# Signs taken in the copy out of PSUM, quarters added by TensorE, in a kernel of window attention and product keys

## What is computed

```
x = L0_attn_hidden_states
xn = _layernorm(x, axis=-1)
s = _L0_attn_ref(xn, ...)
g = _silu(_L0_ffn_ref(xn, L0_ffn_Wq, L0_ffn_keys, L0_ffn_W_down, L0_ffn_W_up))
x = x + s * g
```

```
sx, ix = jax.lax.top_k(sim[0], TOPK)
sy, iy = jax.lax.top_k(sim[1], TOPK)
all_scores = (sx[..., :, None] + sy[..., None, :]).reshape(b, n, HEADS, TOPK * TOPK)
scores, pk_indices = jax.lax.top_k(all_scores, TOPK)
h = jax.nn.gelu(jnp.einsum('bnd,bnhkd->bnhk', x, W_down[pk_indices]), approximate=False)
h = h * jax.nn.softmax(scores, axis=-1)
return jnp.einsum('bnhk,bnhkd->bnd', h, W_up[pk_indices])
```

## Time and profile before

| | us |
|---|---|
| time, median of 3 runs | 278.73 |
| lowest and highest | 277.35, 278.85 |
| the profiled execution, its time | 277.19 |
| its span in the profile | 275.4 |

### The profile page before, as it was taken

How to read it: one execution, slowest core, us unless ns; L and a number is a source line. 1 busy time by engine, 2 the same in 40 slices (tenths; PEclk the granted TensorE clock), 3 DMA queues, 4 the chain that set the end, 5 groups by cost and what they waited for, 6 DMA issues and landing times.

```text
span 275.4 us, 7038 instructions
## 1 busy us (share of the span) xinstructions
PE 237.8 (86%) x1562; PEld 176.2 (64%) x1562; DVE 261.0 (95%) x1715; ACT 234.9 (85%) x1048; POOL 225.9 (82%) x344
## 2 busy tenths in 40 slices
PE   7799689897989988988898889988998899898891
PEld 7456343685668666765676577657765776587780
DVE  5899999999999999999999999999999999998985
ACT  2553866989899999999989999999999999998953
POOL 7889701467588979998999889988998899889972
PEclk9999999999899999999999999999999999999997
DMA  7930000000000000100000000100010001000102
GB/s 179 281 80 1 2 0 0 2 1 0 5 0 0 5 0 1 38 6 0 2 12 31 1 0 2 42 0 5 0 39 4 1 0 40 2 1 4 38 4 76
DMA packets 11228, 6.23 MB, mean 23 GB/s; under 512 B 1457, under 2 KB 10674, under 8 KB 11186
## 3 DMA queue, kind: packets, MB, share of 16 engines
q1 hardware_dynamic: 9858, 5.12, 7.0%
q10 hardware_dynamic: 1328, 0.66, 1.1%
HBM read 3.67 MB, written 2.10 MB: 21 GB/s over the span
## 4 chain that ended last, share of the span: by engine, by line
POOL 29%; PE 29%; ACT 22%; issue 14%; DVE 5%; POOLq 0%; ACTq 0%; DVEq 0%
POOL past L487 4%; PE scratch L1662 4%; PE sim L1570 4%; POOL squareT L502 4%; ACT prob L847 3%; POOL drop L509 3%; POOL wgt L515 3%; PE s_bank L1764 3%; PE s_bank L1758 2%; ACT gap L769 2%; ACT spare L866 2%; PE t_bank L1588 2%; PE s_bank L1553 2%; POOL wgt L523 2%; ACT side L739 2%
## 5 line engine op out<-in xcount | busy, mean ns | idle before, releaser
L1215 DVE MAX8 top<-rest 128x8 f32<-128x40 f32 x512 | 57.4, 191 | 0.1
L1165 DVE MAX8 top<-sim 128x8 f32<-128x32 f32 x496 | 54.0, 184 | 0.0
L847 ACT ACTIVATE prob<-drop 128x50 f32<-128x50 f32 x224 | 51.5, 254 | 0.0
L847 ACT ACTIVATION_READ_ACCUMULATOR prob<-drop 128x1 f32 x224 | 46.9, 211 | 0.0
L502 POOL TENSOR_TENSOR squareT<-sideT 100x512 bf16<-100x512 bf16 x31 | 32.6, 1050 | 4.8 <-ACT sideT L757 4.8
L487 POOL TENSOR_TENSOR past<-gap,last 128x400 f32<-128x400 f32 x31 | 26.8, 864 | 9.5 <-DVE last L1239 9.5
L1570 PE MATMUL sim<-sim_w,xT_all 128*128 128x512 f32 x64 | 33.9, 611 | 0.5 <-ACT xT_all L794 0.5
L509 POOL TENSOR_TENSOR drop<-gap,out_by 128x400 f32<-128x400 f32 x30 | 31.0, 1033 | 1.2 <-ACT out_by L746 1.2
L1588 PE MATMUL t_bank<-gaps_of,topT 128*128 128x200 f32 x128 | 30.1, 359 | 2.0 <-ACT topT L762 2.0
L515 POOL TENSOR_TENSOR wgt<-prob,rden 128x400 f32<-128x400 f32 x30 | 25.7, 856 | 5.9 <-DVE rden L1157 5.9
L1239 DVE MAX8 last<-slot_gap 128x8 f32<-128x22 f32 x256 | 24.4, 169 | 1.1
(11 more groups left out here) (295 smaller groups left out, 755.7 us busy)
## 6 DMA issues: line engine op xcount, KB each, us to landing
out<-y_sb SPq DMA_DIRECT2D x7, 256.0 KB, 2.3
x_sb<-in_L_attn_hidden_states SPq DMA_DIRECT2D x2, 256.0 KB, 3.8
fwq_sb<-in_L_ffn_Wq ACTq DMA_DIRECT2D x2, 256.0 KB, 5.6
x_sb<-in_L_attn_hidden_states SPq DMA_DIRECT2D x1, 512.0 KB, 5.3
wc_sb<-in_L_attn_Wc SPq DMA_DIRECT2D x1, 256.0 KB
out<-last_y SPq DMA_DIRECT2D x2, 128.0 KB, 1.9
wo_in<-in_L_attn_Wo SPq DMA_DIRECT2D x1, 192.0 KB
keys_sb<-in_L_ffn_keys ACTq DMA_DIRECT2D x1, 128.0 KB, 3.3
```

Source lines behind the costliest of these rows:

```text
L847: last = nc.scalar.activation(prob[d][:, h, :], drop[:, h, :], ACT.Exp, scale=-1.0, accum_out=den[d][:, h:h + 1])
L1165: last = nc.vector.max(top[n % 3][:, v, 0:8], sim_bank[n % 2][:, bass.ts(v, KEYS)])
L1215: last = nc.vector.max(top[n % 3][:, v, 8:16], rest[:, v, :])
```

## The change

The sign is no longer taken on its own. GpSimd writes the differences as bf16, TensorE turns the differences themselves, and ScalarE's copy out of PSUM takes the sign (Sign in the place of Copy). side_of goes, with its 32 calls in ScalarE's order and its semaphore. Since the differences stay in use until TensorE has turned them, past_of waits for sideT_ready where it waited for side_done. For the last tile, last_past_of reads the gaps from the PSUM bank in which they still lie (t_bank), and not from their copy; last_squares squares the signs in SBUF and waits for them, where it squared the copy's source in PSUM.

add_quarters goes, with its 28 calls and its semaphore. add_halves has two buffers in turn, and expert_weights adds the two halves that are left with two fp32 matmuls into the same place of PSUM, as it did before for tile 28.

```
-        past = sb("past", [P, HEADS, CANDS])
-        side = sb("side", [P, HEADS, CANDS], BF16)
+        past = sb("past", [P, HEADS, CANDS], BF16)
-        wgt4 = sb("wgt4", [P, HEADS // 2, CANDS])
-        wgt2 = [sb(f"wgt2_{i}", [P, 2, CANDS]) for i in range(2)]
+        wgt4 = [sb(f"wgt4_{i}", [P, HEADS // 2, CANDS]) for i in range(2)]
...
                 pool.wait_ge(last8_done, n + 1)
                 if n >= 1:
-                    pool.wait_ge(side_done, n)
+                    pool.wait_ge(sideT_ready, n)
...
             def add_halves(n):
                 pool.wait_ge(wgt_done, n + 1)
-                w = wgt[n % 2]
-                nc.gpsimd.tensor_tensor(wgt4[:, :, :], w[:, 0:HEADS // 2, :], w[:, HEADS // 2:HEADS, :],
-                                        ALU.add).then_inc(wgt4_done, 1)
-
-            def add_quarters(n):
-                pool.wait_ge(wgt4_done, n + 1)
                 if n >= 2:
                     pool.wait_ge(c_ready, n - 1)
-                nc.gpsimd.tensor_tensor(wgt2[n % 2][:, :, :], wgt4[:, 0:2, :], wgt4[:, 2:4, :],
-                                        ALU.add).then_inc(wgt2_done, 1)
+                w = wgt[n % 2]
+                nc.gpsimd.tensor_tensor(wgt4[n % 2][:, :, :], w[:, 0:HEADS // 2, :], w[:, HEADS // 2:HEADS, :],
+                                        ALU.add).then_inc(wgt4_done, 1)
...
-            def side_of(n):
-                if n < TILES - 1:
-                    act.wait_ge(past_done, n + 1)
-                else:
-                    act.wait_ge(last_past, 1)
-                if n >= 1:
-                    act.wait_ge(sideT_ready, n)
-                nc.scalar.activation(side[:, :, :], past[:, :, :], ACT.Sign).then_inc(side_done, 1)
...
-                    nc.scalar.activation(last_sideT[0:TWO, :], t_bank[0:TWO, :], ACT.Copy).then_inc(sideT_out, 1)
+                    nc.scalar.activation(last_sideT[0:TWO, :], t_bank[0:TWO, :], ACT.Sign).then_inc(sideT_out, 1)
...
-                nc.scalar.activation(sideT[0:TWO, :], f_bank[0:TWO, :], ACT.Copy).then_inc(sideT_out, 1)
+                nc.scalar.activation(sideT[0:TWO, :], f_bank[0:TWO, :], ACT.Sign).then_inc(sideT_out, 1)
...
             def last_squares():
-                nc.scalar.activation(last_squareT[0:TWO, :], t_bank[0:TWO, :], ACT.Square).then_inc(last_square, 1)
+                act.wait_ge(sideT_out, TILES)
+                nc.scalar.activation(last_squareT[0:TWO, :], last_sideT[0:TWO, :], ACT.Square).then_inc(last_square, 1)
...
             def last_past_of(m):
                 dve.wait_ge(last8_done, m + 1)
-                dve.wait_ge(side_done, m)
-                nc.vector.tensor_tensor(past[:, :, :], gap[m % 4][:, :, :],
+                dve.wait_ge(sideT_ready, m)
+                nc.vector.tensor_tensor(past[:, :, :],
+                                        t_bank[:, 0:HEADS * CANDS].rearrange("p (h c) -> p h c", c=CANDS),
                                         last8[m % 2][:, :, 7:8].to_broadcast([P, HEADS, CANDS]),
                                         ALU.subtract).then_inc(last_past, 1)
...
             def transpose_sides(n):
-                pe.wait_ge(side_done, n + 1)
+                if n < TILES - 1:
+                    pe.wait_ge(past_done, n + 1)
+                else:
+                    pe.wait_ge(last_past, 1)
...
-                    last = mm(dst[0:TWO, bass.ts(k, P)], side[:, 2 * k:2 * k + 2, :].rearrange("p h c -> p (h c)"),
+                    last = mm(dst[0:TWO, bass.ts(k, P)], past[:, 2 * k:2 * k + 2, :].rearrange("p h c -> p (h c)"),
                               ident16[:, :], start=True, stop=True)
...
-                if n < TILES - TB:
-                    pe.wait_ge(wgt2_done, n + 1)
-                    last = nc.tensor.transpose(o, wgt2[n % 2][:, :, :].rearrange("p h c -> p (h c)"), ident[:, :])
+                if n <= TILES - TB:
+                    pe.wait_ge(wgt4_done, n + 1)
+                    w, heads = wgt4[n % 2], HEADS // 2
...
+                for h in range(0, heads, 2):
+                    last = mm(o, w[:, h:h + 2, :].rearrange("p h c -> p (h c)"),
+                              ident[:, :], start=(h == 0), stop=(h == heads - 2))
                 last.then_inc(c_ready, 1)
```

More of the change, by code:

```diff
@@ L277, in program @@
         topT_ready, topT_out, gap_ready, gap_out = (sem(n) for n in ("topT_ready", "topT_out", "gap_ready", "gap_out"))
-        slot_gap_done, last8_done, past_done, side_done = (
-            sem(n) for n in ("slot_gap_done", "last8_done", "past_done", "side_done"))
+        slot_gap_done, last8_done, past_done = (sem(n) for n in ("slot_gap_done", "last8_done", "past_done"))
         ahead_done, count_q_done, count_full, count_in = (
@@ L286, in program @@
         half_out = sem("half_out")
-        wgt_done, wgt4_done, wgt2_done, c_ready, c_out = (
-            sem(n) for n in ("wgt_done", "wgt4_done", "wgt2_done", "c_ready", "c_out"))
+        wgt_done, wgt4_done, c_ready, c_out = (
+            sem(n) for n in ("wgt_done", "wgt4_done", "c_ready", "c_out"))
         last_past, last_square, last_kept, last_wgt, blocks_scaled = (
@@ L615, in turn @@
                     add_halves(n - 4)
-                    add_quarters(n - 4)
                     square_of(n - 2)
@@ L819, in _ @@
             take_topT(1)
-            side_of(0)
             take_gaps(1)
@@ L991, in turn @@
                     take_topT(n - 1)
-                    side_of(n - 2)
                     if b >= 2:
@@ L1054, in _ @@
             take_sides(0)
-            side_of(1)
             unit(0, U_KW, [(kw[:, :], 0, bk_sb, 1.0)])
@@ L1070, in _ @@
             out_by_of(TILES - 3)
-            side_of(TILES - 2)
             unit(B - 1, U_VW, [(vw[:, :], 0, bv_sb, 1.0)])
@@ L1076, in _ @@
             window_exps(B - 1, range(LAST, TB))
-            side_of(TILES - 1)
             block_exps(B - 1)
@@ L1627, in expert_weights @@
                 o = dst[0:TWO, bass.ts(n % TB, P)]
-                if n < TILES - TB:
-                    pe.wait_ge(wgt2_done, n + 1)
-                    last = nc.tensor.transpose(o, wgt2[n % 2][:, :, :].rearrange("p h c -> p (h c)"), ident[:, :])
-                else:
[L1632 to L1643, removed]
+                if n <= TILES - TB:
+                    pe.wait_ge(wgt4_done, n + 1)
+                    w, heads = wgt4[n % 2], HEADS // 2
+                elif n < TILES - 1:
+                    pe.wait_ge(wgt_done, n + 1)
+                    w, heads = (wgt if n < TILES - LAST else last_wgts)[n % 2], HEADS
+                else:
+                    pe.wait_ge(last_wgt, 1)
+                    w, heads = last_wgts[n % 2], HEADS
+                for h in range(0, heads, 2):
+                    last = mm(o, w[:, h:h + 2, :].rearrange("p h c -> p (h c)"),
+                              ident[:, :], start=(h == 0), stop=(h == heads - 2))
                 last.then_inc(c_ready, 1)
```

## The result

The changed kernel takes 276.31 us (median of 22 executions, 276.11 to 279.26), the kernel before in the same comparison 278.64 us (22 executions, 277.22 to 280.07). The ratio is 0.9931 with a 95% interval of 0.9913 to 0.9949, or -2.3 us between the medians where -1.0 was forecast. The lowest times lie 1.1 us apart and the two profiled executions 0.66 us (276.53 and 277.19). So the first question is which of these is the change's.

A forecast was written before the change was run, and what follows sets the result against it. A lap of waits round ScalarE, TensorE and GpSimd, not VectorE, was taken to bound the kernel. Laps -0.1, way in -0.4 and tail -0.5 gave -1.0 us: median 277.7 us, own range 276.6 to 278.5, full range 275.0 to 279.9.

The forecast's parts named there:

- The lap: Main loop, one batch element in four turns round ScalarE, TensorE and GpSimd: -0.02 us each, -0.1 us over six.
- Sign at turn 1: ScalarE in turn 1: without side_of, pT_win comes 0.43 us earlier.
- Stall at turn 0: TensorE at turn 0: transpose_sides no longer waits for ScalarE, -0.25 us, between 0.19 and 0.30.
- expert_weights in turn 1: TensorE's unbroken stretch in turn 1: the extra matmuls adding the quarters cost +0.33 us.
- In turn 3: TensorE between the count and the block scores: the extra matmuls of expert_weights cost +0.33 us.
- VectorE's floor: Main loop: VectorE's busy time of 27.52 us per 28.15 us period; its 0.63 us of waiting limits the gain.
- the freed loop: Rival for the main loop: TensorE's extra 0.66 us hides, VectorE alone binds, 274.0 us; chance 0.18, partly or in full.
- The way in: Loop's first turns: the 0.51 us wait for side_of goes, part is given back; -0.4 us, between 0 and -0.9.
- The tail: End of kernel: last_past_of falls from 1.62 to 0.56 us, part is lost; -0.5 us, between 0 and -1.06.
- The Sign from PSUM at nothing: ScalarE's copy out of PSUM: taking Sign there was priced at nothing; 50 ns dearer would be 0.1 us.
- TensorE as the bound: Rival at turn 1: matmuls delay the pair gaps, 0.43 us isn't won while 0.66 is paid; 280.7 us, chance 0.14.
- the change's own wait: Rival at the end: waits for tile 30's transposes and in last_squares eat the gain; 278.7 us, chance 0.21.

The follow-up runs named there:

- the faster mixed kernel: Changed kernel with add_quarters put back on GpSimd for turns 1 and 3, TensorE adding in turns 0 and 2: 272.27 us, ratio 0.9827.
- experiments 1 and 2: No edit: 1 is the kernel before beside itself, 277.49 us, ratio 0.9964; 2 is the changed kernel once more, 276.40 us, ratio 0.9909.
- experiment 12: Changed kernel with tile 31's differences read from ScalarE's SBUF copy again instead of PSUM: 276.34 us, ratio 0.9928.
- experiments 9 and 10: Kernel before with throw-away matmuls in the loop's first turn 1: eight in 9, 277.30 us; five in its early part in 10, 277.21 us.
- experiments 3, 5 and 6: Changed kernel with add_quarters back on GpSimd: all turns in 3, 273.10 us; turns 1 and 3 in 5, 272.27; turns 0 and 2 in 6, 276.14.
- experiment 4: Kernel before with add_quarters removed and TensorE adding the quarters, nothing else of the change: 281.67 us, ratio 1.0089.
- the kernel of turn 2: Kernel before with three throw-away TensorE matmuls of 0.24 us per lap in turn 2, ahead of the count: 277.35 us, ratio 0.9993.

## Why the prediction was right, and what it left out

**The bound** was right, and the experiments show it: the sides without the quarters are 3.3 us faster than both together, the quarters without the sides 2.9 us slower than before at full clock.

**The lap.** Each term was measured within 0.04 us. Sign at turn 1: from the turn 0 transposes to pT_win 8.88 us before (172.99 to 181.87), 8.47 after (172.75 to 181.22), -0.41 for -0.43. Stall at turn 0: 0.51 to 0.26 us between the starts, -0.25 for -0.25. expert_weights in turn 1: pT_win to row squares 6.56 before, 6.89 after, +0.33 for +0.33. In turn 3: 0.48 between the starts of expert_weights and of the matmul behind it (170.12 to 170.60) for 0.11 (170.47 to 170.58), +0.37 for +0.33. The sum is +0.04 instead of -0.02, and the row squares are 28.15 to 28.20 us apart in the two traces of the changed kernel, 28.14 to 28.16 in the two of the kernel before. The transposes of turn 0, before first:

```profile
172.99 0.43 PE L1600 MATMUL f_bank<-ident,side 128*100 128x128 bf16 x4 [0.19 <-ACT side L739]
```

```profile
172.75 0.42 PE L1573 MATMUL f_bank<-ident,past 128*100 128x128 bf16 x4
```

What the sum couldn't tell is that the terms don't simply add: the extra matmuls of turn 3 and the stall of turn 0 lie behind one another, so alone the matmuls cost 0.46 and not 0.66.

**VectorE's floor** of the freed loop was set 0.05 to 0.15 us too high. The prediction took 27.52 us, VectorE's busy time in the kernel before; in the faster mixed kernel a period is 27.37 to 27.47 and VectorE busy 27.23 of 27.37. And with the sides alone not VectorE but GpSimd binds, at 27.64, through the very quarters that I had priced at nothing. They cost nothing while another engine binds; with two of the four taken off GpSimd the steady lap falls by 0.17 us (row squares 27.47 apart). The chain of the kernel before had shown them ahead of past_of and the Sign of turn 0:

```profile
198.06 0.40 POOL wgt L530
```

**The way in.** From the last pair gaps ahead of the loop to the first row squares it was 25.71 us (without a fall) or 25.87 before, 25.04 and 25.05 after: -0.67 to -0.82, where I took -0.4 and gave -0.9 as the bound. I had subtracted what the fallen clock would take back; in the traces of the changed kernel it did not fall. The executions of experiments 1 and 2:

```profile
50.38 0.94 PE L1588 MATMUL t_bank<-gaps_of,topT 128*128 128x200 f32 x4 [0.87 <-ACT topT L762]
...
76.09 0.28 ACT L866 ACTIVATE spare<-s_bank 128x128 f32<-128x128 f32 x1 [0.51 <-PE s_bank L1764]
```

```profile
50.52 0.94 PE L1558 MATMUL t_bank<-gaps_of,topT 128*128 128x200 f32 x4 [0.87 <-ACT topT L739]
...
75.56 0.28 ACT L842 ACTIVATE spare<-s_bank 128x128 f32<-128x128 f32 x1 [0.51 <-PE s_bank L1733]
```

**The tail** was -0.4 for -0.5. last_past_of did as forecast: its end came 0.65 us earlier, counted from the last row squares, for -0.74. But of that 0.15 to 0.3 arrive (experiment 12).

**The Sign from PSUM at nothing** was right: the copy took 607 ns as Copy in the kernel before and takes 607 ns as Sign. Both rows, before first:

```profile
L757 ACT ACTIVATE sideT<-f_bank 100x512 bf16<-100x512 f32 x31 | 18.8, 607 | 0.7 <-PE f_bank L1600 0.5
```

```profile
L734 ACT ACTIVATE sideT<-f_bank 100x512 bf16<-100x512 f32 x31 | 18.8, 607 | 5.6 <-PE f_bank L1573 5.5
```

**The step that was mis-sized** is the last one, from the profiled execution to the median. I wrote that the profiled execution lay 1.54 us below the median and carried these 1.54 over to the changed kernel. They were no constant of the chip but the price of the fallen clock in 57 of 98 executions, and the change mostly removes it. That filling the first turn 1 removes the falls is shown by experiments 9 and 10; that the sides' part of the change does so too, by experiments 3, 5 and 6 (a fallen clock in 2 of 22 executions without the waits for the Sign) beside experiment 4 (in 4 of 7 with the quarters alone). By which of the waits that went with it, is not shown. In the stretch of 64 to 68 us the kernel before waits 0.65, 0.45 and 0.52 us (experiment 1's execution) and the changed kernel 0.45 and 0.38; the one that went is the wait for VectorE's slot_gap, before first:

```profile
65.63 0.41 PE L1579 MATMUL t_bank<-ident,top 128*128 128x128 f32 x2 [0.65 <-DVE slot_gap L1230]
```

```profile
65.53 0.41 PE L1549 MATMUL t_bank<-ident,top 128*128 128x128 f32 x2
```

The earlier trace rows showed the fall before the prediction; I priced it inside one execution and did not ask what it does to the others. Between the executions of experiments 1 and 2 the terms measured add up to -1.0 (way in -0.7, laps -0.1, tail -0.4, a later prologue +0.1), and at full clock the kernels are 0.9 to 1.0 apart. The first two profiled executions lie only 0.66 apart because the prologue of the changed one ended 0.49 us later; over the traces of both kernels and of their variants, but for experiment 4's, that end scatters between 50.2 and 50.8 us.

**What was luck.** That the sum came out at -1.0 is partly chance: the way in gave 0.3 more than forecast, and the tail, the laps and the scatter of the prologue took that back. And the median measured, 276.31 us, lies outside the forecast's own 276.6 to 278.5, in the part of the full range that was there for the freed loop; the freed loop did not come, and the clock filled its place. The other number, 276.2 us from the profiled execution's own time, was met by 276.31.

The rivals: the freed loop did not come, since the matmuls don't hide in turns 1 and 3; TensorE as the bound did not come, since the pair gaps kept the 0.31 us of slack; the change's own wait ate part of the tail's gain, not all.

On the two pages of the Trainium skill: "SBUF — State Buffer", section "Who interferes with whom", has a VectorE operation with two SBUF inputs exclude a GpSimd one that reads SBUF. The runs agree: 1.23 us with the SBUF operand and 0.57 with the PSUM operand, beside the same 1.27 us, and GpSimd's square behind that takes 1.38 and 1.04. "VectorE: DVE Perf Modes", section on the TRN2 errata, charges a PSUM source some 65 ns more, an estimate; the 0.57 us here stand beside 0.557 us of another operation with a PSUM operand, and no run here has the same operation undisturbed from SBUF, so that stays open.

## What to carry to other kernels

Follow the lap, not the shares: the same extra matmuls cost 0.33 us in a turn where TensorE works without a break and nothing in one where it waits, so a change that helps on one engine and hurts on another is best taken turn by turn (here 272.3 us instead of 276.1). When the runs of a kernel spread over 1%, look at the granted clock of each execution before taking their median as the base of a forecast. And waits that cost nothing on the path can still decide whether TensorE's clock holds behind them: filled in experiments 9 and 10, they left the full-clock time where it was, at 277.2 to 277.3 us.

## What was not expected of the hardware

The granted clock fell in 57 of 98 executions of one and the same program and stayed up in the others; with five short matmuls in one stretch of 4 us it fell in 0 of 12, with eight in 1 of 12. What decides from one execution to the next, no run here shows. A fall costs as much as what stands on the path there: in the earlier trace rows 0.16 us on the way in (25.87 for 25.71 us), in the kernel of turn 2 about 1 us (26.68 us on the same way), and in the kernel with the quarters alone, where a fall came in turn 1 of a later lap, one lap of 30.1 instead of 28.61 us.
